# Merging a grouped attention's set-up blocks, loading by need, and moving the expert outputs' gathers and weight fetches

## The chip, the cores and the metric

The kernel runs on one core of one Trainium2 chip, as one launch. The metric is the device time of that launch in microseconds. Runs of the same kernel agree closely here: the three runs of the kernel before lie between 3903.95 and 3909.45 us.

A core has five engines with queues of their own: PE (TensorE, matmul), DVE (VectorE), ACT (ScalarE), POOL (GpSimd) and SP (SyncE, which here only issues transfers). They meet through semaphores. Each queue is worked in order, so an instruction that waits holds up everything behind it on its engine.

## The reference, cut to what matters

The input `x` is 4 batches of 256 tokens of 256 numbers; `ctx_2048` is 4 batches of 1601 rows of 256. Eight layers run one after the other, each as `x = x + layer(layernorm(x))`:

```python
x = x + _L0_xattn_ref(...)      # top-k memory attention
x = x + _L0_ffn_ref(...)        # 8 gelu experts, top 2 of them for each token
x = x + _L1_xattn_ref(...)      # grouped attention with rope
x = x + _L1_ffn_ref(...)        # linear
x = x + _L2_xattn_ref(...)      # image and text attention
x = x + _L2_ffn_ref(...)        # capacity experts
x = x + _L3_xattn_ref(...)      # grouped attention without rope
x = x + _L3_ffn_ref(...)        # silu experts
```

The gelu experts (`_L0_ffn_ref`): a softmax over 8 gates, and for each token the two largest, then

```python
h = gelu(x @ W1 + b1);  h = gelu(h @ W2 + b2);  eo = h @ W3 + b3
out = sum over the two chosen experts of  gate weight * eo
```

A grouped attention (`_L1_xattn_ref`, `_L3_xattn_ref`): 16 query heads of 128, 4 key and value heads. Queries come from `x`, keys and values from the context (in layer 1 from context and `x` together, 1857 rows). Queries and keys are RMS-normalised; layer 1 turns them by position (rope). Then softmax(q k / sqrt(128)) v, and the output projection.

## The kernel before

**Stages.** The layers are the stages a0, f0, a1, f1, a2, f2, a3, f3, and each consists of blocks. A block is a program for each engine; at its end all engines meet at a barrier, the semaphores are cleared, and they meet again. `x` stays in on-chip memory (`m.x`, in the profile `x_slots`) as 8 tiles of 128 tokens. The context lies in device memory as two halves, `ctx_hi` and `ctx_lo`, since each product is made of three products of high and low parts.

**f0, the gelu experts** (`gelu_experts`). The router gives each of the 2048 pairs (token, expert) a slot. POOL scatters the normalised rows to `z_slots` in device memory (L1665, 16 transfers), after which 15 blocks of 256 slots are worked (L1727, L1743, L1759 are the three layers' matmuls). For each block SP loads the rows (L1687, `f_zb`) and POOL fetches the expert's weights by index (L1641, 2.1 MB, three buffers). POOL fetches the weights of block 0 ahead of the scatters and those of blocks 1 and 2 directly behind them; then it rounds a third of block 0's weights (L1651), and DVE makes the low part of it (L1848) ahead of the low part of the first rows (L1853), which the first matmul needs. SP stores each block's results to `y_slots` (L1697). When all are stored, still in the same block, POOL gathers 16 tiles (expert choice `k`, token tile `t`) back (L1678, `got`, eight buffers), and DVE adds each to `x` times its gate weight (L1934).

**a1 and a3, the grouped attentions** (`grouped_attention`). Each has four blocks.

- `_once`: SP loads the norms' weights, the first weights and (in a1) the frequencies (L762) and waits for all; POOL sets constants (L768 to L774).
- `_first`: prepares batch 0's first key and value head. SP loads the whole context of batch 0 (L831, 1.6 MB for each half), then in a1 the positions (L822 to L826), then the tokens (L844, `a_x_n`). The order of work on the other engines is one list, `FIRST_TASKS`.
- `_groups`: 16 groups (4 batches of 4 heads) of 30 turns (a1) or 26 (a3). The list `GROUP_TURNS` says what is done beside the attention proper in each turn: the next head's keys and values, and so on.
- `_last`: the last output projection.

**Tasks** in the lists, a letter code with a number: `V` and `W` split weights into high and low; `PR`, `PX`, `RA` and `RS` make the table of sines and cosines from the positions (DVE L1353, L1357, L1370 to L1387, ACT L1136); `N`, `NZ`, `NX` normalise tokens; `KV t` is keys and values of context tile t (PE L929, ACT L1086 and L1088, DVE L1235); `KN` (POOL L1160 to L1165) and `KR` (DVE L1248 to L1256) normalise and turn four such tiles; `Q`, `QN`, `QR` the same for the queries; `KX` and `QX` transpose; `R` is a rough product of queries and keys and its maximum (PE L1002, DVE L1316, POOL L1188); `NB` spreads the maxima. Every engine does its own part of each task in the order of the list. Items that pass through PSUM (`PX NX KV Q KX QX OX Y NB`) share two banks in turn: item i waits until DVE has freed item i-2.

In `_first` R8 needs all keys (`KX3`), so the block is two parts: everything up to R8, and then R8 to R15 and NB0, which is a chain of PE and DVE alone. Groups begin after that.

## Time and profile before

| | us |
|---|---|
| median of three runs | 3904.76 |
| the runs | 3903.95, 3904.76, 3909.45 |
| the profiled execution | 3914.25 |
| its span, first to last instruction | 3912.1 |
| its mean granted TensorE clock, share of full | 0.936 |
| PE busy | 3534.0 (90%) |
| DVE busy | 2346.7 (60%) |
| ACT busy | 2243.7 (57%) |
| POOL busy | 853.5 (22%) |

The profile is one execution, so sums are made against its own 3914.25 us. Where PE is busy nearly without a break, only less work on PE would help; where PE stands idle, the engine or transfer that is waited for sets the time. On the page the span is cut into 40 slices, and a digit is the busy share of a slice in tenths:

```profile
PE   6756965999999999999599999886999999999989
DVE  8873756676676677664477777433555555555434
PEclk7866986999999999999799999887999999999989
```

### The profile page before, as it was taken

To read this page: it belongs to the slowest core of one execution; us is meant where nothing else is said; L and a number is where in the kernel's file an instruction comes from. 1 tells how busy PE (TensorE), PEld (TensorE's weight loads), DVE (VectorE), ACT (ScalarE), POOL (GpSimd) and SP (SyncE) were. 2 spreads that over 40 slices of the span, in tenths; PEclk is the share of its full clock that TensorE was granted. 3 is DMA by queue.
4 is the path that set the end of the run, shared out by engine and by line. 5 is a ranking of instruction groups with operands and counts; after the bars stand their busy time and mean duration, and the time that the engine had idled before them with its cause. 6 is when DMAs were issued, how large, how long until landed. Compare 5 with 4: busy or idle time off the path is not lost. (4 is left out here: it accounts for less than half of the span.)

```text
span 3912.1 us, 63758 instructions
## 1 busy us (share of the span) xinstructions
PE 3534.0 (90%) x23965; PEld 3018.9 (77%) x23965; DVE 2346.7 (60%) x4208; ACT 2243.7 (57%) x5207; POOL 853.5 (22%) x1073
## 2 busy tenths in 40 slices
PE   6756965999999999999599999886999999999989
PEld 5545964988988888888556666574898998989878
DVE  8873756676676677664477777433555555555434
ACT  3313743667666667666266666513666666666643
POOL 0002122222322222221111220102223232322214
PEclk7866986999999999999799999887999999999989
DMA  3213531010010001000200000101010010010001
GB/s 134 84 41 143 197 116 60 23 54 17 20 59 15 23 20 53 20 6 6 71 35 35 1 35 1 70 35 68 25 54 20 28 54 28 20 56 17 7 29 40
DMA packets 53360, 177.85 MB, mean 45 GB/s; under 512 B 5884, under 2 KB 27840, under 8 KB 46016
## 3 DMA queue, kind: packets, MB, share of 16 engines
q1 hardware_dynamic: 47200, 136.37, 9.9%
q0 software_dynamic: 3696, 35.72, 2.6%
q8 instruction: 192, 3.15, 0.3%
q10 hardware_dynamic: 2160, 1.71, 0.2%
q14 instruction: 112, 0.92, 0.1%
HBM read 145.44 MB, written 24.13 MB: 43 GB/s over the span
## 5 line engine op out<-in xcount | busy, mean ns | idle before, releaser
L1038 PE MATMUL ps<-a_v_rows,a_probs 128*128 128x129 f32 (+1 forms) x7168 | 943.8, 276 | 0.0
L1038 PEld LDWEIGHTS ps<-a_v_rows,a_probs 128*128 128x128 f32 (+1 forms) x7168 | 895.4, 191 | 39.9 <-issue 4.2
L1121 ACT ACTIVATE a_probs<-ps 128x512 f32<-128x512 f32 (+1 forms) x896 | 535.7, 598 | 605.4 <-PE ps L1027 604.4
L1316 DVE TENSOR_REDUCE a_neg<-ps 128x1 f32<-128x1024 f32 (+2 forms) x512 | 540.0, 1056 | 401.2 <-PE ps L1002 400.6
L1131 ACT ACTIVATE ps<-a_negb 128x512 f32<-128x512 f32 (+1 forms) x892 | 536.7, 602 | 58.2 <-DVE a_negb L1331 30.2
L1188 POOL TENSOR_SCALAR a_diag<-ident,a_negmax 128x128 fp32r<-128x128 f32 x256 | 157.9, 617 | 1482.2 <-DVE a_negmax L1324 1480.6
L1023 PE MATMUL ps<-a_qt,a_kt 128*128 128x512 f32 (+1 forms) x896 | 428.4, 478 | 1.4 <-PEq L72 1.4
L929 PE MATMUL ps<-a_wr,a_ct 128*128 128x256 f32 (+1 forms) x2496 | 363.1, 287 | 10.1 <-DVE a_k_rows L1235 7.8
L929 PEld LDWEIGHTS ps<-a_wr,a_ct 128*128 128x128 f32 (+1 forms) x2496 | 335.6, 187 | 37.9 <-DVE a_k_rows L1235 10.2
L1027 PE MATMUL ps<-a_qt,a_kt 128*128 128x512 f32 (+1 forms) x896 | 355.5, 397 | 0.0
L1025 PE MATMUL ps<-a_qt,a_kt 128*128 128x512 f32 (+1 forms) x896 | 354.1, 395 | 0.0
L3238 ACT ACTIVATE a_probs<-ps 128x1024 f32<-128x1024 f32 x224 | 229.6, 1025 | 151.2 <-PE ps L3117 150.8
L1002 PE MATMUL ps<-a_kt,a_qt 128*128 128x512 f32 (+2 forms) x1024 | 292.8, 369 | 13.8 <-DVE a_negmax L1324 6.8
L1235 DVE TENSOR_TENSOR a_k_rows<-ps,a_kw 128x128 f32<-128x128 f32 (+1 forms) x448 | 129.6, 290 | 213.5 <-ACT a_v_rows L1088 201.0
L3416 DVE TENSOR_REDUCE a_parts<-ps 128x1 f32<-128x448 f32 x384 | 222.9, 618 | 46.9 <-PE ps L3079 44.9
L1002 PEld LDWEIGHTS ps<-a_kt,a_qt 128*128 128x128 f32 x1024 | 178.5, 193 | 70.6 <-DVE a_neg L1316 26.7
L1027 PEld LDWEIGHTS ps<-a_qt,a_kt 128*128 128x128 f32 (+1 forms) x896 | 165.7, 185 | 42.9
L1023 PEld LDWEIGHTS ps<-a_qt,a_kt 128*128 128x128 f32 (+1 forms) x896 | 170.0, 190 | 4.8 <-issue 2.8
L1025 PEld LDWEIGHTS ps<-a_qt,a_kt 128*128 128x128 f32 (+1 forms) x896 | 169.2, 189 | 0.8
L3117 PE MATMUL ps<-a_qt,a_kt 128*128 128x512 f32 x448 | 165.0, 450 | 2.2 <-DVE a_qt L3408 1.2
L3079 PE MATMUL ps<-a_kt,a_qt 128*128 128x448 f32 (+1 forms) x512 | 154.6, 371 | 7.5 <-ACT a_kt L3206 1.6
L1161 POOL TENSOR_TENSOR a_k_sq<-a_k_sq,nhalf 128x4 f32<-128x4 f32 (+2 forms) x128 | 151.2, 1181 | 10.7
(461 smaller groups left out, 6048.9 us busy)
## 6 DMA issues: line engine op xcount, KB each, us to landing
a_ct<-ctx_hi SPq DMA_DIRECT2D x12, 1602.0 KB, 6.9
a_ct<-ctx_lo SPq DMA_DIRECT2D x12, 1602.0 KB, 10.6
a_wf<-in_a_wq SPq DMA_DIRECT2D x32, 512.0 KB, 3.5
a_wf<-in_a_wo SPq DMA_DIRECT2D x32, 512.0 KB, 3.5
f_we<-in_f_experts SPq DMA_DIRECT2D x8, 1088.0 KB, 8.7
a_wf<-in_a_wkv SPq DMA_DIRECT2D x32, 256.0 KB, 2.7
ctx_hi<-a_ct SPq DMA_DIRECT2D x4, 1602.0 KB, 5.3
ctx_lo<-a_ct SPq DMA_DIRECT2D x4, 1602.0 KB, 8.8
```

What stands on the lines that cost most here:

```text
L929: ins = pe.matmul(out[0:r, 0:2 * HD], src, wr[0][v][:, c * 2 * HD:(c + 1) * 2 * HD], start=(n == 0), stop=(n == 3 * DC - 1))
L1002: ins = pe.matmul(m.ps[:, rough_at(task) + k, 0:c1 - c0], queries[0][:, j * P:(j + 1) * P], keys[0][:, c0:c1], start=True, stop=True)
L1023: pe.matmul(out, kt[0][:, at:at + r], qt[0][:, cols], start=False, stop=False, skip_group_check=True)
L1025: pe.matmul(out, kt[0][:, at:at + r], qt[1][:, cols], start=False, stop=False, skip_group_check=True)
L1027: pe.matmul(out, kt[1][:, at:at + r], qt[0][:, cols], start=False, stop=True, skip_group_check=True).then_inc(st_ready, 1)
L1038: ins = pe.matmul(m.ps[:, 6 + i // 2, (i % 2) * 256:(i % 2) * 256 + VW], probs[0:r, n % 3, i * P:(i + 1) * P], v_rows[g % 2][0:r, t, :], s ...
L1121: act.activation(probs[0:r, n % 3, :], m.ps[0:r, 4 + n % 2, :], ACT.Exp)\
L1131: act.activation(m.ps[0:r, 4 + n % 2, :], negb[0:r, G, :], ACT.Copy).then_inc(seeded, 1)
L1316: ins = dve.tensor_reduce(neg2[:, j, r % 2:r % 2 + 1], flat2(m.ps[:, rough_at(task):rough_at(task) + 2, :])[:, 0:e - a0], AX.X, ALU.max, n ...
L3117: ins = pe.matmul(m.ps[:, 4 + 2 * (n % 2) + half, :], kt[g % 2][:, half, t * P:(t + 1) * P], qt[g % 2][:, half, :], start=True, stop=True)
L3238: act.activation(flat2(probs[n % 3][:, :, :]), flat2(m.ps[:, first:first + 2, :]), ACT.Exp)\
L3416: dve.tensor_reduce(to, slot(("R", h, j))[:, 0:n], AX.X, ALU.max, negate=True).then_inc(neg_done, 1)
```

## The change

**In f0.** POOL's fetch of block 1's weights waits until the rows of block 0 have landed, and the fetch of block 2's until those of block 1 have. The gathers and additions at the end of f0 are taken out; the slots and the gate weights (one copy on DVE, `share`) are kept for the next stage.

**In a1.** The gathers and additions are done by two new tasks, `GP j` on POOL and `GA j` on DVE, j from 0 to 15, with four buffers (halves of `z` and `x_b`) in place of eight. The first four pairs, which make batch 0's tokens, are in `FIRST_TASKS`; the other twelve are in group 0's turns 8 to 21 of `GROUP_TURNS`.

**In a1 and a3.** The block `_once` is gone; its loads and constants are the head of `_first`. POOL sets only the last context tile of `k_rows`, not all. SP's loads come in a new order, the context in two column parts (512 columns and the rest) with a semaphore each; `KV4` waits for the second. In `_first` the items use four PSUM banks, not two (`_groups` keeps two). `FIRST_TASKS` is another order.

The lists, of which the tables' rows themselves tell little:

```diff
 GROUP_TURNS = {
     True: (
-        "KV4 RA1 R4", "KV5 KV6 KN0 QR3", "R5 KV7 KR0 KN1", "Y0 KR1 KV8 W1 R6", "KV9 KX0", "R7 KV10 KV11 KR2",
...
+        "KV4 RA1 R4", "KV5 KV6 KN0 QR3", "GP4 R5 KV7 KR0 KN1", "GP5 Y0 KR1 KV8 W1 R6", "GP6 KV9 KX0 GA4",
...
 FIRST_TASKS = {
     True: (
-        "V1 V0 PR0 N0 PX0 RA0 RA1 RA2 RA3 NZ0 RA4 NX0 RA5 RA6 RA7 RA8 RA9 Q0 Q1 RS0 KV0 QN0 KV1 KV2 KV3 KV4 QR0 "
...
+        "GP0 V0 GP1 PR0 GP2 PX0 RA0 RA1 RA2 RA3 GA0 RA4 GA1 RA5 RA6 GA2 RA7 GP3 KV0 GA3 RA8 RA9 KV1 KV2 N0 KV3 "
...
     False: (
-        "V1 N0 V0 NZ0 NX0 Q0 Q1 KV0 KV1 KV2 KV3 KV4 KV5 KV6 QN0 KV7 KV8 KN0 QN1 KN1 KV9 KV10 KV11 KV12 QX0 KN2 KX0 "
...
+        "N0 V0 KN0 NZ0 QN0 QN1 KV0 NX0 KV1 V1 KV2 KV3 Q0 Q1 KN1 KX0 KV4 KV5 KV6 KV7 KV8 KV9 KV10 KV11 W1 KN2 QX0 "
```

The code:

```diff
-        with nc.Block(name=f"{name}_once") as block:
-            @block.sync
-            def _(sp):
-                loads = [(qw[:, :], w["qw"].partition_broadcast(P)), (kw[:, :], w["kw"].partition_broadcast(P)),
-                         (wf[0][:, :], w["wkv"][0]), (wf[1][:, :], w["wq"][0])]
...
-                sp.wait_ge(once, 16 * len(loads))
...
+            ITEM_BANKS = (2, 3) if attend else (2, 3, 6, 7)
...
                     if not attend:
-                        load_context(0)
+                        load_weights(KVH - 2, 0)
+                        sp.dma_start(qw[:, :], w["qw"].partition_broadcast(P)).then_inc(norm_in, 16)
+                        sp.dma_start(kw[:, :], w["kw"].partition_broadcast(P)).then_inc(norm_in, 16)
                         if rope:
+                            sp.dma_start(invf[:, :], w["inv_freq"].partition_broadcast(P)).then_inc(norm_in, 16)
+                            sp.wait_ge(zeroed, 1)
                             load_positions(0)
-                        sp.dma_start(x_n[:, :, :], m.x[:, 0:QT, :]).then_inc(x_in, 16)
+                        else:
+                            sp.dma_start(x_n[:, :, :], m.x[:, 0:QT, :]).then_inc(x_in, 16)
+                        load_context(0, 0)
+                        load_weights(KVH - 2, 1)
+                        load_context(0, 1)
+                        if rope:
+                            sp.wait_ge(m.added, 2 * QT)
+                            sp.dma_start(x_n[:, :, :], m.x[:, 0:QT, :]).then_inc(x_in, 16)
...
+                    def GP(g, j):
+
+                        k, t = PAIRS[j]
+                        if j >= 4:
+                            pool.wait_ge(m.added, j - 3)
+                        pool.indirect_dma_start(out=got(j), out_offset=None, in_=m.y_slots,
+                                                in_offset=bass.IndirectOffsetOnAxis(ap=m.slot[:, k, t:t + 1], axis=0))\
+                            .then_inc(m.fetched[j % 4], 16)
...
+                    def GA(g, j):
+
+                        k, t = PAIRS[j]
+                        dve.wait_ge(m.fetched[j % 4], 16 * (j // 4 + 1))
+                        if k:
+                            dve.wait_ge(m.added, j)
+                        dve.scalar_tensor_tensor(out=m.x[:, t, :], in0=got(j), scalar=m.share[:, t, k:k + 1],
+                                                 in1=m.x[:, t, :], op0=ALU.mult, op1=ALU.add).then_inc(m.added, 1)
...
+                    if not attend:
+                        dve.wait_ge(zeroed, ZEROED)
+                        dve.wait_ge(norm_in, 16 * NORMS)
...
+                pool.wait_ge(z_in[0], 16)
                 fetch_weights(1)
+                pool.wait_ge(z_in[1], 16)
                 fetch_weights(2)
...
-                for i in range(2):
-                    pool.wait_ge(y_out[i], 16 * len(range(i, NB, 2)))
-                for j, (k, t) in enumerate(fetches):
-                    if j >= 8:
-                        pool.wait_ge(added, j - 7)
-                    pool.indirect_dma_start(out=got[:, j % 8, :], out_offset=None, in_=m.y_slots,
-                                            in_offset=bass.IndirectOffsetOnAxis(ap=slot[:, k, t:t + 1], axis=0))\
-                        .then_inc(fetched[j % 8], 16)
```

**Where instructions stand on the queues.** First SP, from the end of f0 into a1's first block; in brackets is what an instruction waits for. The kernel before:

```order
L1633 UNCONDITIONAL_BRANCH [waits f0_y_out1,f0_y_out0]
L71 ISA [waits barrier_Pool_Activation_PE_DVE_SP_release] x2
L755 UNCONDITIONAL_BRANCH [waits barrier_Pool_Activation_PE_DVE_SP_release]
L762 DMA a1_qw<-in_a1_qw 128x128
L762 DMA a1_kw<-in_a1_kw 128x128
L762 DMA a1_wf0<-in_a1_wkv 128x512
L762 DMA a1_wf1<-in_a1_wq 128x1024
L762 DMA a1_invf<-in_inv_freq 128x64
L754 UNCONDITIONAL_BRANCH [waits a1_once]
L71 ISA [waits barrier_Pool_Activation_PE_DVE_SP_release]
L818 UNCONDITIONAL_BRANCH [waits barrier_Pool_Activation_PE_DVE_SP_release]
L831 DMA a1_ct0<-ctx_hi 128x3204
```

The changed kernel, SP at the same place:

```order
L805 UNCONDITIONAL_BRANCH [waits barrier_Pool_Activation_PE_DVE_SP_release]
L826 DMA a1_wf0<-in_a1_wkv 128x512
L831 DMA a1_qw<-in_a1_qw 128x128
L832 DMA a1_kw<-in_a1_kw 128x128
L834 DMA a1_invf<-in_inv_freq 128x64
L809 DMA a1_pos_i<-in_pos 12x128 [waits a1_zeroed]
L811 DMA a1_pos_i<-in_pos 1x65
L813 DMA a1_pos_i<-in_tok 2x128
L820 DMA a1_ct0<-ctx_hi 128x2x512
L820 DMA a1_ct1<-ctx_lo 128x2x512
L826 DMA a1_wf1<-in_a1_wq 128x1024
L820 DMA a1_ct0<-ctx_hi 128x2x1090
```

The barrier between the two lists of loads is gone, and the positions stand ahead of the context; before, they stood behind both of its loads.

Next POOL in f0, from the scatters on (`expert_in0` is the arrival of block 0's weights). Before:

```order
L1665 DMA z_slots<-f_z,f_slot 3840x256 x15
L1641 DMA f_wf<-in_f_experts,f_of 128x4104 x2
L1651 CAST f_wr<-f_wf 128x1024 [waits expert_in0]
L1651 CAST f_wr<-f_wf 128x1024 [waits f0_h_ready,expert_in1]
L1641 DMA f_wf<-in_f_experts,f_of 128x4104 [waits f0_hi_done,f0_w_lo]
```

And in the changed kernel:

```order
L1701 DMA z_slots<-f_z,slot 3840x256 x15
L1677 DMA f_wf<-in_f_experts,f_of 128x4104 [waits f0_z_in0]
L1677 DMA f_wf<-in_f_experts,f_of 128x4104 [waits f0_z_in1]
L1687 CAST f_wr<-f_wf 128x1024 [waits expert_in0]
L1687 CAST f_wr<-f_wf 128x1024 [waits f0_h_ready,expert_in1]
```

The two fetches now wait for rows (`z_in`), and the rounding of block 0's weights, which waits for neither, stands behind them.

Last POOL in group 0 of a1, turns 7 to 13 (the three lines on `a_k_sq` and `a_k_rows` are one `KN`, the line on `a_diag` is an `R`). Before:

```order
L1165 TENSOR_TENSOR a_k_rows<-a_k_rows,a_k_sq 128x512
L1188 TENSOR_SCALAR a_diag<-ident,a_negmax 128x128
L1160 TENSOR_SCALAR a_k_sq<-a_k_sq 128x4
L1161 TENSOR_TENSOR a_k_sq<-a_k_sq,nhalf 128x4
L1165 TENSOR_TENSOR a_k_rows<-a_k_rows,a_k_sq 128x512
L1188 TENSOR_SCALAR a_diag<-ident,a_negmax 128x128
L1160 TENSOR_SCALAR a_k_sq<-a_k_sq 128x4
L1161 TENSOR_TENSOR a_k_sq<-a_k_sq,nhalf 128x4
```

And changed:

```order
L1170 TENSOR_TENSOR a_k_rows<-a_k_rows,a_k_sq 128x512
L1201 DMA a_z<-y_slots,slot 128x256
L1193 TENSOR_SCALAR a_diag<-ident,a_negmax 128x128
L1165 TENSOR_SCALAR a_k_sq<-a_k_sq 128x4
L1166 TENSOR_TENSOR a_k_sq<-a_k_sq,nhalf 128x4
L1170 TENSOR_TENSOR a_k_rows<-a_k_rows,a_k_sq 128x512
L1201 DMA a_z<-y_slots,slot 128x256
L1201 DMA a_x_b<-y_slots,slot 128x256 x2
L1193 TENSOR_SCALAR a_diag<-ident,a_negmax 128x128
L1201 DMA a_z<-y_slots,slot 128x256 x2
L1165 TENSOR_SCALAR a_k_sq<-a_k_sq 128x4
```

Six gathers now stand among two `KN` and two `R` steps; the two directly ahead of the last `KN` shown are GP8 and GP9, and GP9 waits for the addition GA5 on DVE.

## Rows read from the trace of the kernel before

**Rows 1.** Busy time by stretch: from:to, length, engines' busy, clock, DMA share, GB/s

```profile
core 0: us, PE busy (x) PEld busy (x) DVE busy (x) ACT busy (x) POOL busy (x), PEclk, DMA share, GB/s
340.00:355.00 15.00, 0.64 (x3) 0.67 (x4) 1.22 (x1) 0.00 (x0) 2.81 (x3) 0.50 0.84 324
556.00:581.00 25.00, 0.00 (x0) 0.00 (x0) 7.75 (x16) 0.00 (x0) 15.16 (x16) 0.52 0.29 84
589.30:665.80 76.50, 38.59 (x149) 28.08 (x149) 49.26 (x85) 20.26 (x75) 17.99 (x22) 0.63 0.15 57
```

**Rows 2.** Timeline, f0's first rows: start, length, engine, line, [idle before, releaser]

```profile
339.82 0.98 POOL L1641 DMA_INDIRECT f_wf<-in_f_experts,f_of  x1 [0.30 <-issue]
340.96 14.87 SPq L1687 DMA_DIRECT2D f_zb<-z_slots  x3
342.07 1.05 POOL L1651 CAST f_wr<-f_wf 128x1024 fp32r<-128x1024 f32 x1
343.16 1.22 DVE L1848 TENSOR_TENSOR f_wr<-f_wf,f_wr 128x1024 fp32r<-128x1024 f32 x1 [13.55 <-POOL f_wr L1651]
354.36 1.09 PE L1712 MATMUL ps<-ident,f_zb 128*128 128x128 f32 x4 [27.48 <-DMA f_zb<-z_slots]
356.95 5.46 PE L1727 MATMUL ps<-f_zt_b,f_wr 128*128 128x256 f32 x24 [1.50 <-DVE f_zt_b L1853]
...
365.32 1.07 ACT L1803 ACTIVATE f_wr<-f_wf 128x1024 fp32r<-128x1024 f32 x1
```

**Rows 3.** Line L1687, the 15 loads of rows: time to landing

```profile
DMA to landing us min/median/max: 2.6/6.6/13.4
```

**Rows 4.** Timeline, the end of f0 and the start of a1

```profile
556.41 0.97 POOL L1678 DMA_INDIRECT f_got<-y_slots,f_slot  x1 [18.16 <-DMA y_slots<-f_yb]
...
559.22 0.48 DVE L1934 SCALAR_TENSOR_TENSOR x_slots<-f_got,f_top,x_slots 128x256 f32<-128x256 f32 x1 [5.23 <-DMA f_got<-y_slots,f_slot]
...
577.96 0.48 DVE L1934 SCALAR_TENSOR_TENSOR x_slots<-f_got,f_top,x_slots 128x256 f32<-128x256 f32 x1 [0.82 <-DMA f_got<-y_slots,f_slot]
581.02 0.35 SPq L762 DMA_DIRECT2D a_qw<-in_a_qw  x1
...
582.84 0.43 SPq L762 DMA_DIRECT2D a_invf<-in_inv_freq  x1
```

**Rows 5.** Line L762, the nine loads of both once blocks: time to landing

```profile
DMA to landing us min/median/max: 2.9/4.5/5.8
```

**Rows 6.** Timeline, a1's first block

```profile
601.00 0.21 DVE L1353 CAST a_pos_rows<-a_pos_i 15x128 f32<-15x128 int32 x1 [8.68 <-DMA a_pos_i<-in_tok]
...
602.86 1.17 DVE L1370 TENSOR_TENSOR a_ang_tmp<-a_pos_f,a_invf 128x960 f32<-128x960 f32 x1
```

**Rows 7.** Busy time from first angle (a1) or token statistics (a3) to R8

```profile
602.86:650.72 47.86, 28.21 (x130) 22.91 (x130) 34.31 (x62) 17.81 (x73) 14.64 (x18) 0.71 0.00 1
2669.86:2700.66 30.80, 20.63 (x116) 16.25 (x116) 12.45 (x31) 14.17 (x64) 13.19 (x18) 0.83 0.08 26
```

**Rows 8.** Transfers by line, whole span: issues, KB each, median us to landing

```profile
a_x_n<-x_slots SPq DMA_DIRECT2D x8, 256.0 KB, 2.3
```

**Rows 9.** Timeline, a3's once and first blocks

```profile
2650.54 0.33 SPq L762 DMA_DIRECT2D a_qw<-in_a_qw  x1
...
2669.86 0.75 DVE L1222 BATCH_NORM_STATS2 a_stats<-a_x_n 128x6 f32<-128x256 f32 x2 [9.75 <-DMA a_x_n<-x_slots]
```

**Rows 10.** Busy time in group 0 of a1

```profile
665.90:734.00 68.10, 67.99 (x454) 61.13 (x455) 43.58 (x76) 47.90 (x125) 19.36 (x24) 0.97 0.12 40
```

**Rows 11.** Timeline, one KN on POOL in group 0 of a1

```profile
700.93 0.19 POOL L1160 TENSOR_SCALAR a_k_sq<-a_k_sq 128x4 f32<-128x4 f32 x1
...
702.75 1.04 POOL L1165 TENSOR_TENSOR a_k_rows<-a_k_rows,a_k_sq 128x512 f32<-128x512 f32 x1
```

**Rows 12.** Timeline in f0, a weight fetch beside DVE's splits

```profile
422.27 0.95 POOL L1641 DMA_INDIRECT f_wf<-in_f_experts,f_of  x1 [0.48 <-issue]
422.48 2.36 DVE L1848 TENSOR_TENSOR f_wr<-f_wf,f_wr 128x1024 fp32r<-128x1024 f32 x2 [0.40 <-ACT f_wr L1803]
```

109 lines of the change are left out of this document (58 added, 51 removed), and 9 rows, old and new, of tables (FIRST_TASKS, GROUP_TURNS).

## The prediction

> **What bounds the kernel now.** I read the busy shares by slice first: PE is at nine tenths in most slices, and the dips lie between stages. So the time is PE's work plus the stretches in which PE stands still, and the change touches three of these. The table of busy time by stretch [rows 1] shows them: 15 us at the start of the experts in which PE does 0.64 us of work; 25 us at their end with none; and a1's first block, 76.5 us with PE at 38.6 and DVE at 49.3. The timelines then say what each waits for.
>
> In the first [rows 2], SP issues block 0's rows at 340.96, and PE starts on them at 354.36: a wait of 13.4 us, in which the DMA engines move 324 GB/s on average [rows 1], nearly all of it the two weight fetches issued from 339.82. The same load takes 2.6 us at best and 6.6 in the middle of the 15 [rows 3].
>
> In the second [rows 4], POOL has waited for the last store until 556.41, gathers 16 tiles one after the other, and DVE adds the last at 577.96. Next comes the once block from 581.02, whose loads must all land before the first block begins. There the angles begin only at 602.86, because the positions, queued behind 3.2 MB of context, are used first at 601.00 [rows 6]. The a3 stage shows the same: from 2650.54 to the first use of the tokens at 2669.86 nothing but loads is on the path [rows 9].
>
> **Part 1, the weight fetches.** With the rows alone in flight they land 2.6 us after 340.96, at 343.6. This releases POOL, which issues both fetches (0.97 each and 0.3 between: to 345.9) and only then rounds block 0's third part (1.05, to 347.0); DVE's low part follows (1.22, to 348.3), and only behind it the low part of the rows. From the rows' arrival PE needed 356.95 - 354.36 = 2.59 us to its first expert matmul [rows 2], so the rows' own chain would be done at 346.2; the rounding is the later one. With an estimated 0.7 for the rows' low part, a transfer-free piece of that 2.59, the first matmul starts at 349.0, against 356.95: **-7.9**. The new wait holds back, on POOL, both fetches and the rounding, and PE waits for all three in the end. Block 1's weights now start 3.8 us later and land, if both share the engines as they did, some 13 us after 343.6, at 357. ACT splits them first at 365.32 [rows 2], 357.4 when 7.9 is taken off, so there is no margin: up to 3 us can be lost here. One copy on DVE (`share`) adds about 0.2. Part 1: **-7.7**, between -9 and -4.
>
> **Part 2, the end of f0 and the start of a1.** From the last addition's end, 577.96 + 0.48 = 578.44, to the next block's first instruction took 2.6 us [rows 4]. Without the tail the same barriers start when the last store has landed, at 556.4 (the cause of POOL's release), so a1 begins at 559.0 in place of 581.02: **-22.0**. This holds within 0.5 us, since it is an interval of the trace with its content taken out.
>
> From a1's first load to the first angle it was 602.86 - 581.02 = 21.8 us. Now frequencies are the fourth load, 1.4 us after the start at the measured spacing of 0.45, and the norms' loads took 2.9 to 5.8 us to land, 4.5 in the middle [rows 5]. DVE waits for all of them before anything else: 5.9. Then a split half as wide as the 1.22 one of [rows 2], some 0.7, and the cast, transposition and copy of the positions, at most the 602.86 - 601.00 = 1.9 us that they took with the tokens' statistics between [rows 6], say 1.2: the angles begin 7.8 us in. **-14.0**, between -12.5 and -16. The positions are issued by about 3 us, and are tiny, so they aren't last; the context is behind them now, and KV0 needs only its first 512 columns. The four gathers issue on POOL while it has nothing else to do, 1.25 us each, and land before DVE, busy with angles, asks for them: no cost but their additions.
>
> From the first angle to R8 it was 47.86 us, with DVE busy 34.31 and PE 28.21 [rows 7]: neither is full, it is a chain that passes between them. DVE gets four additions (4 x 0.48), two splits of 1.2 that stood outside this stretch and the tokens' statistics (0.75 [rows 9] and small steps, some 1.2): 5.5 more, 39.8. If DVE were never idle, the stretch would be 39.8 (-8.0); if its idle 13.55 us stayed as they are, 53.4 (+5.5). The new order fills some of that idle time: KV0 to KV3 run on PE under the angles, where PE was waiting, and four banks let PE run ahead of DVE. Against it: tokens now wait for the fourth addition and a 2.3 us copy [rows 8], and Q comes late, so that POOL's QN and KN1 follow one another. I followed DVE's list by hand with the durations of this trace and came to 46; it is near the middle, and I take **-2.0**. R8 to the groups' start keeps its work.
>
> **Part 3, a3.** From the once block's first load to the tokens' use it was 19.3 us [rows 9]. Now the tokens are the fourth load (1.4 us in) ahead of the context; the copy takes 2.3 us alone [rows 8] and up to the 5.8 of such loads behind 384 KB. I take 5.5 in all: **-13.8**, between -12 and -15. From there to R8 it was 30.8 us with PE at 20.63 and DVE at 12.45 [rows 7]. Two banks made PE wait for DVE; four don't. One split (1.2) comes in. From PE's floor (-10) to the same idle time (+1.2); I take **-2.0**, nearer to the upper end, because Q, its norm on POOL and the keys' norms behind it on POOL are still one chain.
>
> **Part 4, group 0 of a1.** PE is busy 67.99 of 68.10 us there, DVE 43.58, POOL 19.36 [rows 10]. Twelve gathers take POOL 12 x 0.95 and twelve additions DVE 12 x 0.48 = 5.8 us. Both have room, but the queues are in order. Most exposed is KN2, which ran from 700.93 to 703.79 [rows 11]: POOL must now first issue GP8 and GP9, and GP9 waits for GA5 on DVE, which stands behind KR2. That puts KN2 about 3 us later, DVE's KR4 behind it 1 to 2 us, and PE's next item behind DVE about 1. With a similar smaller slip elsewhere: **+2**, between 0 and +9 (every addition on the path, and KN2's 3 us).
>
> **A rule against part 4.** The fetch at 422.27 kept its 0.95 us on POOL although DVE worked on a split, two operands from SBUF, from 422.48 for 2.36 us [rows 12]. The Trainium skill ("SBUF — State Buffer", section "SBUF: two separate sides") says that a transfer issued from GpSimd needs descriptors written by GpSimd, and that DVE, while it holds the shared port pair in a two-port mode, keeps GpSimd from writing them; so the transfer waits for the end of DVE's instruction. By it, gathers issued among DVE's rope products would each come up to a DVE instruction late, which is the second rival's direction; in the row the issue itself isn't longer. The sum stays with the row.
>
> **Sum:** -7.7 - 22.0 - 14.0 - 2.0 - 13.8 - 2.0 + 2 = **-59.5 us**. On the profiled 3914.25 that is 3854.8. The median of the runs is 9.5 us lower than the profiled execution, and no row ties this difference to the changed places, so I take the same sum off the median: 3904.76 - 59.5 = **3845.3**.
>
> **Rivals.**
> 1. *The rows are late for another reason than the weights* (the scatters just before them write the same memory). Then the fetches, which now wait for the rows, start at 354.4, the rounding ends 3.4 us later, and the first matmul comes at 359.8: +2.9 in place of -7.7. Time 3855.9. Against it: the 324 GB/s, and the 2.6 us of an undisturbed load. 5%.
> 2. *Group 0 pays for each gather.* POOL is in order, and PE follows DVE closely: if each of twelve gathers costs PE its issue and gap, 1.25 us, part 4 is +15. Time 3858.3. For it: PE has no slack at all [rows 10]. Against it: POOL and DVE have. 8%.
> 3. *Slower: the ring of four runs empty.* If DVE reaches each GA before its gather has landed, it waits for a whole round: from POOL's issue to DVE's start 2.8 us, the addition 0.48, 0.3 of issue [rows 4], and where a KN or R stands between on POOL its 2.9 as well [rows 11]. This is 6.5 us for each of twelve, 78 in all, PE behind it: 3904.76 - 61.5 + 78 = 3921. It decides from 61.5 / 12 = 5.1 us for each. Against it: the turns are 2.3 us long (68.1 / 30) and GA stands two turns behind its GP, with three more gathers in flight. 2%.
> 4. *The first blocks gain nothing in their order*: the idle time stays (+5.5 and +1.2 in place of -2.0 twice), 3856. Within my range, part of the forecast.
>
> **How the numbers follow.** The forecast with its unknown terms has 83%, the rivals 5, 8 and 2, and 2 for what I don't see. The terms' ends add up to gains between 40 and 75 us if not all fall to one side: 3830 to 3865, which holds rivals 1 and 2; I give 3832 to 3864. A change of 0.2% (7.8 us) is about what a measurement of this kernel can tell from none. Faster by more: 0.97; within: 0.01; slower: 0.02.
>
> **What would show it.** In the profile after: block 0's rows landing 2.6 to 4 us after their issue, and PE's first expert matmul about 8 us after that issue (16 before); POOL's rounding behind both fetches; no gathers ahead of the barrier, and a1's first load 2.6 us behind the last store's landing; the first angle 8 us later; R8 about 54 us after a1's first load (69.7 before) and, in a3, about 34 (50.1 before); KN2 in group 0 ending some 3 us later in its group, and the group 2 us longer than 68. Wrong would be: a stall of ACT on block 1's weights, DVE waiting at the start of the first block for norms' loads over 7 us, a longer stretch from angles to R8, or DVE waiting on gathers in group 0.

## The result and the profile after

The changed kernel takes 3838.14 us (median of 4 runs, 3836.81 to 3841.64), the kernel before 3904.36 beside it (3903.17 to 3909.45). The ratio is 0.9829, 95% interval 0.9812 to 0.9846: 66.2 us, or 1.7%, less. Forecast were 59.5 less (3845.3). The profiled execution took 3837.82, with a span of 3836.1.

Its timeline where f0's experts start answers to [rows 2]. Columns are start, length, engine, line, operation, and in brackets the idle time before and its releaser:

```profile
336.13 4.17 SPq L1717 DMA_DIRECT2D f_zb<-z_slots  x3
338.82 1.09 PE L1742 MATMUL ps<-ident,f_zb 128*128 128x128 f32 x4 [16.78 <-DMA f_zb<-z_slots]
338.95 0.98 POOL L1677 DMA_INDIRECT f_wf<-in_f_experts,f_of  x1 [4.26 <-DMA f_zb<-z_slots]
340.23 0.96 POOL L1677 DMA_INDIRECT f_wf<-in_f_experts,f_of  x1 [0.30 <-issue]
341.20 1.04 POOL L1687 CAST f_wr<-f_wf 128x1024 fp32r<-128x1024 f32 x1
342.28 1.23 DVE L1878 TENSOR_TENSOR f_wr<-f_wf,f_wr 128x1024 fp32r<-128x1024 f32 x1 [17.51 <-POOL f_wr L1687]
343.42 0.68 DVE L1883 TENSOR_TENSOR f_zt_b<-ps,f_zt_b 128x512 fp32r<-128x512 f32 x1
344.25 4.74 PE L1757 MATMUL ps<-f_zt_b,f_wr 128*128 128x256 f32 x24 [4.34 <-DVE f_zt_b L1883]
...
351.92 1.07 ACT L1833 ACTIVATE f_wr<-f_wf 128x1024 fp32r<-128x1024 f32 x1
```

The rows are in PE's hands 2.7 us behind their issue, where they took 13.4. What remains until the first expert matmul is POOL's list: two fetches, one rounding, then DVE's two low parts. Block 1's weights land 8.6 us behind their fetch's issue, at 347.6, and ACT splits them from 351.92, without a wait.

The end of f0 and the start of a1 answer to [rows 4] and [rows 6]:

```profile
540.55 0.36 SPq L1727 DMA_DIRECT2D y_slots<-f_yb  x1
543.82 0.35 SPq L826 DMA_DIRECT2D a_wf<-in_a_wkv  x1
...
549.28 0.69 DVE L1226 TENSOR_TENSOR a_wr<-a_wf,a_wr 128x512 fp32r<-128x512 f32 x1 [8.76 <-DMA a_invf<-in_inv_freq]
550.58 0.21 DVE L1387 CAST a_pos_rows<-a_pos_i 15x128 f32<-15x128 int32 x1 [0.60 <-DMA a_pos_i<-in_tok]
551.38 1.15 DVE L1404 TENSOR_TENSOR a_ang_tmp<-a_pos_f,a_invf 128x960 f32<-128x960 f32 x1
```

No gather stands ahead of the barrier, and the angles begin 7.56 us behind a1's first load. Busy time by stretch: the first two rows answer to [rows 7] (first angle to R8 in a1, token statistics to R8 in a3), the third to [rows 10] (the first 68.1 us of group 0). Columns as in [rows 1]:

```profile
551.38:593.86 42.48, 25.24 (x130) 21.84 (x130) 37.81 (x71) 18.32 (x73) 16.65 (x18) 0.70 0.29 106
2596.34:2624.89 28.55, 17.53 (x112) 15.57 (x112) 13.01 (x32) 14.07 (x64) 14.17 (x18) 0.80 0.43 155
608.57:676.67 68.10, 66.06 (x434) 58.88 (x435) 47.31 (x85) 46.14 (x122) 32.90 (x35) 0.96 0.19 63
```

DVE is now busy 37.81 of 42.48 us in a1's first stretch, where it stood idle for 13.55 us before. In group 0, PE has lost 1.9 us.

I cut both traces, and later those of the experiments, at the same events. All values are lengths in us, the difference of two starts read in the timeline (B and C meet at the end of the last copy of outputs):

| stretch | before | changed | difference | forecast |
|---|---|---|---|---|
| A rows' issue to first expert matmul | 15.99 | 8.12 | -7.9 | |
| B to the last output copy's end | 197.03 | 196.27 | -0.8 | A and B: -7.7 |
| C to a1's first load | 27.04 | 3.30 | -23.7 | -22.0 |
| D to the first angle | 21.84 | 7.56 | -14.3 | -14.0 |
| E to R8 | 47.86 | 42.48 | -5.4 | -2.0 |
| F to the groups' first score | 15.19 | 14.71 | -0.5 | 0 |
| G to a1's last score | 1200.89 | 1202.47 | +1.6 | +2 |
| H a3's first load to token statistics | 19.32 | 4.64 | -14.7 | -13.8 |
| I to R8 | 30.80 | 28.55 | -2.3 | -2.0 |
| J to the groups' first score | 15.08 | 14.18 | -0.9 | 0 |

These add up to -68.8. The spans differ by 76.0; the other 7.2 lie where nothing was changed: everything ahead of the rows' issue took 4.8 us less, a1's last score to a3's first load 3.1 less, and what follows a3's first score 0.7 more. Over the 14 traces of this study these two stretches vary from 336.1 to 341.4 and from 776.8 to 785.0 us, so they say nothing about a change. The profiled execution of before (3914.25) lay 9.9 us above its median, that of the changed kernel 0.3 below; the medians, 66.2 apart, are the measure.

### The profile page after: what moved, and what is told of

It is laid out like the page before. It is cut to its first block and busy times, and to the rows that moved or that the text cites. A ratio compares the mean times of both kernels' runs of the same rounds, so it can differ in the third digit from the quotient of the medians.

```text
span 3836.1 us, 63738 instructions
## 1 busy us (share of the span) xinstructions
PE 3525.6 (92%) x23965; PEld 3014.9 (79%) x23965; DVE 2343.7 (61%) x4209; ACT 2240.2 (58%) x5207; POOL 855.4 (22%) x1073
## 3 DMA queue, kind: packets, MB, share of 16 engines
q1 hardware_dynamic: 53600, 136.37, 10.1%
```

## The experiments

All were run beside the kernel before, which took 3909.7 to 3911.4 us there; so ratios are compared, and stretches by the letters above. A second profile of the changed kernel says how exact a stretch is.

**The changed kernel again.** 

> The changed kernel once more, beside the combined version on the same chip. Its ratio to the kernel before should fall in 0.981 to 0.985, and the stretches of its trace should agree with the first profile's within 1 us: 8.1 us from the rows' issue to the first expert matmul, 64 to 66 from a1's first load to its groups, 1202.5 for them, 47.4 from a3's first load to its groups. If a stretch differs by more, differences of that size in the other experiments mean nothing.

Median 3842.70, ratio 0.9823 (0.9809 to 0.9836). A 8.20, B 196.03, C 3.30, D 7.73, E 42.29, F 14.72, G 1202.68, and a3's H to J together 47.23 where the first profile had 47.37. These stretches repeat within 0.4 us (H and I each for itself shift by 0.4 and 0.5, their sum by 0.1). In the experiments below D varies between 7.3 and 8.5 without an edit to it, so D is good to about 1 us. Where the interval of a ratio overlaps the repeat's, as in all experiments but 3, 4 and 5, it is the stretches that tell, not the time.

**1. The weights in front of the rows.** 

> The changed kernel without POOL's two waits for the first rows: weight fetches 1 and 2 are issued right behind the scatters, as before the change. Theory (the small load of rows is served in turns with 4 MB of weights): rows land 12 to 14 us after their issue instead of 2.7, the first expert matmul comes 16 us behind the issue instead of 8.1, the time is 7 to 9 us above the changed kernel's, about 3846. Rival (the rows were late because of the scatters just ahead of them, and come early in the changed kernel for another reason): they land in about 3 us here too, and the time stays at 3838.

```diff
-                pool.wait_ge(z_in[0], 16)
                 fetch_weights(1)
-                pool.wait_ge(z_in[1], 16)
                 fetch_weights(2)
```

Ratio 0.9837 (0.9818 to 0.9857). The timeline of its start:

```profile
338.73 15.38 SPq L1715 DMA_DIRECT2D f_zb<-z_slots  x3
...
352.63 1.08 PE L1740 MATMUL ps<-ident,f_zb 128*128 128x128 f32 x4 [28.00 <-DMA f_zb<-z_slots]
...
355.22 5.03 PE L1755 MATMUL ps<-f_zt_b,f_wr 128*128 128x256 f32 x22 [1.50 <-DVE f_zt_b L1881]
```

The rows take 13.9 us again, and A is 16.49, 8.3 more than in the repeat. Everything else is as in the changed kernel. The rival (the scatters make the rows late) falls: the scatters stand ahead of them in both kernels, and only the two waits differ. The ratios alone, 5 us apart, with intervals that overlap, couldn't have told it.

**2. The once block put back.** 

> The changed kernel with a once block put back ahead of the heads' first block in all grouped attentions (norms' weights, first key and query weights, frequencies, memsets, all waited for, then a barrier); the order of the other loads and of the tasks stays. Theory (the order of the loads did most of the work in a1, the second wait and barrier the rest): in a1 the first angle comes 11 to 12 us behind the first load (7.6 in the changed kernel, 21.8 before), in a3 the tokens' statistics 10 to 11 us behind it (4.6; 19.3 before), in all +9 us, about 3847. Rival (the once block itself was the cost): a1 back at over 18 us and a3 at over 16, in all +22 or more.

```diff
+        with nc.Block(name=f"{name}_once") as block:
+            @block.sync
+            def _(sp):
+                loads = [(qw[:, :], w["qw"].partition_broadcast(P)), (kw[:, :], w["kw"].partition_broadcast(P)),
+                         (wf[0][:, :], w["wkv"][0]), (wf[1][:, :], w["wq"][0])]
...
+                sp.wait_ge(norm_in, 16 * len(loads))
...
+        st.clear()
```

The block also sets all of `k_rows` again, as before the change. D is 11.22 (+3.5 on the repeat), H 10.29 (+5.3); the ratio is 0.9839 (0.9823 to 0.9856), median 3847.45. So the wait for all loads and the barrier are worth 9 us in the two stages together. The remaining 20 of D and H are taken to come from what stands ahead of what; this is a remainder, not a run of its own.

**3. The gathers back in f0.** 

> The changed kernel with all 16 gathers and additions put back at the end of the experts' block, as before; everything else stays. Theory (the tail was a serial stretch of its own and its work costs little inside a1): from the last store's issue to a1's first load 26 to 27 us instead of 3.3, the first block of a1 1 to 2 us shorter, group 0 of a1 1.5 us shorter, in all +20 to +22, about 3859. Rival (the gathers cost a1 several us, which other gains hide): a1's first block and group 0 become over 5 us shorter and the whole is under +17.

The edit puts POOL's wait for `y_out`, its 16 gathers and DVE's 16 additions back behind the loop over blocks, and takes all GP and GA out of a1's lists.

Ratio 0.9877 (0.9861 to 0.9894), 0.0054 or 21 us above the repeat. C is 27.04, exactly that of before. D is 7.26, E 39.72 (2.6 less than the repeat), F 15.07, G 1201.65 (1.0 less). The tail was worth 23.7 us, and its work costs a1 2.7 us in the first block (D to F), more than the 1 to 2 expected and than the additions alone, which were all I had counted, and 1.0 us in G; group 0 by itself lost more than that, as part 4 below shows.

**4. The first tasks in nearly the old order.** 

> The changed kernel with the heads' first tasks in nearly the order they had before the change (both splits first, queries ahead of the keys), the four first gathers and additions ahead of the tokens; loads, banks and all else stay. Theory A (the new order fills DVE's and PE's idle time): the stretch from the first angle to R8 in a1, 42.5 us in the changed kernel, goes to 48 to 52, and in a3 the stretch from the tokens' statistics to R8, 28.6 us, grows by 2 to 4: in all +8 to +12. Theory B (the shorter stretch comes from the four banks, the new order does nothing of its own): both stay within 1.5 us.

```diff
-        "GP0 V0 GP1 PR0 GP2 PX0 RA0 RA1 RA2 RA3 GA0 RA4 GA1 RA5 RA6 GA2 RA7 GP3 KV0 GA3 RA8 RA9 KV1 KV2 N0 KV3 "
...
+        "GP0 V1 GP1 V0 PR0 GP2 PX0 RA0 RA1 RA2 RA3 GA0 RA4 GA1 RA5 RA6 GA2 RA7 GP3 GA3 N0 RA8 RA9 NZ0 NX0 "
+        "Q0 Q1 RS0 KV0 QN0 KV1 KV2 KV3 KV4 QR0 "
...
```

In a1 this is not the old list exactly: the tokens' tasks N0, NZ0 and NX0 stand behind RA7, since the tokens are now loaded last.

Ratio 0.9880 (0.9863 to 0.9896): 22 us above the repeat, twice what theory A expected; theory B falls. D is 15.70, E 54.17, F 15.21: from a1's first load to its groups 85.1 us, against 84.9 in the kernel before. With nearly the old order, all that the loads, the banks and the single block gain in a1 is lost to the four gathers and to waits. In a3 H is 13.20 and H to J 55.69 (+8.5); the stretch in which theory A looked for a3's loss, I, did not grow (27.40). Two rows of its timeline show how:

```profile
559.61 1.83 DVE L1227 TENSOR_TENSOR a_wr<-a_wf,a_wr 128x1024 fp32r<-128x1024 f32 x2 [16.45 <-ACT a_wr L1074]
...
580.69 5.25 PE L948 MATMUL ps<-a_wr,a_zt 128*128 128x512 f32 x12 [1.50 <-DVE a_zt L1240]
```

V1, the split of the query weights, is DVE's first task. Its weights are loaded behind 1 MB of context (two parts of 512 KB), so DVE stands until 559.61, 13.2 us behind the first load; in the changed kernel the positions are in use 6.8 us behind it. Then PE's first large work is Q, at 580.69, at the lower clock. In the changed kernel Q comes behind keys:

```profile
569.78 2.99 PE L947 MATMUL ps<-a_wr,a_zt 128*128 128x512 f32 x12
```

The busy time of these two intervals, the changed kernel's first, then this one's; the third number from the end is the granted clock:

```profile
569.78:572.77 2.99, 2.99 (x15) 2.40 (x15) 1.76 (x6) 1.68 (x11) 0.00 (x0) 0.99 0.27 101
```

```profile
580.69:585.94 5.25, 5.25 (x14) 4.14 (x15) 0.69 (x1) 1.15 (x8) 0.00 (x0) 0.53 0.00 0
```

0.99 is the level of 2.4 GHz; 0.53 is for the most part that of 1.2. Ahead of 580.69 PE had been busy for 1.4 of the 19.7 us since 561.00; ahead of 569.78 it had been busy for 11.5 of the 15.5 us since 554.26. The same twelve matmuls take 2.3 us more at the lower clock. In the kernel before they took as long as in this one:

```profile
610.14 5.29 PE L944 MATMUL ps<-a_wr,a_zt 128*128 128x512 f32 x12 [1.58 <-DVE a_zt L1216]
```

**5. Old order and gathers in f0.** 

> Both undone at once: the heads' first tasks in nearly the old order, and all gathers back at the end of the experts' block; the single block, the loads by need and the four banks stay. Theory (the old order is bad only because the tokens now come late, behind four additions, and Q stands ahead of the keys): from a1's first load to its groups 73 to 78 us, against 84.9 before, 85.1 with the old order and gathers in a1, and 62.1 with the new order and no gathers. Rival (the old order costs as much without gathers): 82 to 85.

The edits are those of 3 and 4 together. Ratio 0.9930 (0.9915 to 0.9945). D 14.47, E 49.77, F 15.54: 79.8 us, between theory and rival. DVE stands for V1 here as well. The four corners for a1's first load to its groups are then:

| | gathers in f0 | gathers in a1 |
|---|---|---|
| nearly the old order | 79.8 | 85.1 |
| new order | 62.1 | 64.8 |

With the new loads, the order is worth 17.7 us without gathers and 20.3 with them. Loads by need, the single block and four banks together, with nearly the old order, are worth 84.9 - 79.8 = 5.1. The new order with the old loads was not run.

**6. Two banks.** 

> The changed kernel with two banks of PSUM for the items of the heads' first block instead of four. Theory A (four banks let PE run ahead of DVE and are part of the gain): from the first angle to R8 in a1 3 to 6 us longer than 42.5, from the tokens' statistics to R8 in a3 2 to 3 us longer than 28.6, in all +5 to +9. Theory B (the order alone does it, the chain passes through POOL and DVE): both within 1 us of the changed kernel.

```diff
-            ITEM_BANKS = (2, 3) if attend else (2, 3, 6, 7)
+            ITEM_BANKS = (2, 3)
```

Ratio 0.9844 (0.9828 to 0.9861). E 48.92 (+6.6), a3's H to J 49.22 (+2.0). Theory A holds, with 0.6 more in a1 than expected and less in a3's I (+1.5 for 2 to 3). The table of PE's waits shows the mechanism; in this kernel, from 556 to 605 us (line waited for: us in total, times, longest):

```profile
PE ps L932 <- DVE a_k_rows L1267: 8.9, 6, 3.9
```

and in the changed kernel, from 551 to 594:

```profile
PE ps L932 <- DVE a_k_rows L1267: 1.6, 2, 1.1
```

PE's keys wait until DVE has emptied a bank: DVE is busy with the angles, and with four banks the program lets PE work up to four tiles ahead of it.

**7. POOL's rounding ahead of the waits.** 

> The changed kernel with POOL's rounding of block 0's third part ahead of both waits for rows, where in the changed kernel it stands behind both fetches. Theory (POOL's fetch, fetch, rounding and then DVE's two low parts are the chain to the first expert matmul): that matmul comes 5.3 to 5.7 us behind the rows' issue instead of 8.1, the time falls by 2.5 to 3, about 3835.5. Rival (PE then waits for block 1's weights or for the clock, so the start is given back): the first matmul is earlier, but from the rows' issue to f0's last copy of outputs stays 204.4 us.

```diff
+                split_third(0)
                 pool.wait_ge(z_in[0], 16)
                 fetch_weights(1)
...
-                    split_third(b)
+                    if b:
+                        split_third(b)
```

Ratio 0.9815 (0.9799 to 0.9832). A is 5.42, B 197.16; together 202.6 against 204.2 in the repeat. The matmul comes 2.8 us earlier as expected, and in this trace 1.1 us of that are lost again in B; in two later versions with the same edit A and B are 201.3 and 201.8, a gain of 2.4 to 2.9. What took them here stays open.

**8. A smaller first load of the context.** 

> The changed kernel with the first load of the context cut from 512 columns to 256 and 256, each with its own semaphore. Theory (PE stands still for the context's low part first: 3.1 and 1.6 us in a1, to 9.5 us behind the first load in a3): KV0 starts about 3 us earlier in a1 and 4 us earlier in a3, and R8 comes 1 to 3 us earlier in a3, up to 1 us in a1, where DVE's list is full: -2 to -4 in all. Rival (the chain through the tokens, Q and POOL's norm sets R8): KV0 is earlier and R8 is not, within 0.5 us.

```diff
-                        cols = slice(0, 512) if part == 0 else slice(512, CTXP)
+                        cols = (slice(0, 256), slice(256, 512), slice(512, CTXP))[part]
...
```

Ratio 0.9818 (0.9800 to 0.9837). In a3 PE starts its keys 6.96 us behind the first load, not 9.2 to 9.5, and H to J is 44.82 (-2.4). In a1 they start at 9.14 (9.6 and 10.4 in the two profiles of the changed kernel), and E stays at 42.26: there DVE is the one that is full. This is what a load by need left over. In the changed kernel's a3 the wait moved from the tokens to the context:

```profile
2596.34 0.75 DVE L1254 BATCH_NORM_STATS2 a_stats<-a_x_n 128x6 f32<-128x256 f32 x2 [5.36 <-DMA a_x_n<-x_slots]
...
2601.19 1.62 PE L932 MATMUL ps<-a_wr,a_ct 128*128 128x256 f32 x6 [12.05 <-DMA a_ct<-ctx_lo]
```

**9. Group 0's gathers later, two per turn.** 

> The changed kernel with the twelve gathers and additions of group 0 moved from turns 8 to 21 to turns 15 to 22, behind KN2 and KN3, and the copy of x behind them. Theory (KN2 behind the gathers on POOL costs group 0 its 1.6 us): KN2 ends 38 us behind the groups' start (42 in the changed kernel), and from the groups' start in a1 to its last score it takes 1200.9 as before instead of 1202.5: -1 to -2 us. Rival (each gather and addition costs PE wherever it stands): the stretch stays at 1202.5 or grows, since two gathers stand in each turn.

```diff
-        "GP11 KN3 QX1 GA9", "GP12 KR6 KX1 KR7 KX2 GA10", "GP13 RA3 RA4 GA11", "GP14 KX3 GA12", "GP15 RA5 GA13",
...
+        "KN3 QX1 GP4 GP5", "GP6 KR6 KX1 KR7 KX2 GP7", "GP8 RA3 RA4 GA4 GA5 GP9", "GP10 KX3 GA6 GA7 GP11",
+        "GP12 RA5 GA8 GA9 GP13", "GP14 R8 GA10 GA11 GP15", "R9 RA6 GA12 GA13", "R10 RA7 RA8 GA14 GA15",
```

Ratio 0.9826 (0.9810 to 0.9842): no gain and no loss. Its profile shows G at 1208.02, 5.3 more than the repeat, with one hole: ACT stands until 672.16, DVE until 673.57, PE until 674.84, and what released them is not in the trace:

```profile
672.16 0.60 ACT L1125 ACTIVATE a_probs<-ps 128x512 f32<-128x512 f32 x1 [3.06 <-remote]
...
673.57 1.22 DVE L1351 TENSOR_REDUCE a_neg<-ps 128x1 f32<-128x1024 f32 x1 [4.36 <-remote]
```

No other profile here has such a hole. PE stands 4.5 us in it, and from 672 to 680 us the granted clock is 0.60. The profiled execution was also the longest of the four (3852.31 against a median of 3843.75), so G tells nothing. Up to the hole the theory holds: KN2 ends 38.5 us behind the groups' start, as expected, and POOL's product of KN3 starts at 44.4, where it starts at 44.5 without gathers (experiment 3) and at 48.3 in the changed kernel. Whether the gathers then cost PE something in their new turns this run can't say; the next two can.

**10. A combined version.** 

> Four things on top of the changed kernel: POOL's rounding of block 0's third part ahead of the waits for rows; the context's first 512 columns in two loads; in a1 the frequencies and positions are the first loads, the positions' cast and angles stand ahead of the first split, which alone waits for the norms; group 0's gathers one per turn in turns 14 to 25 with their additions two to three turns behind, the copy of x last. Expected: first expert matmul 5.4 us behind the rows' issue (8.1), in a1 the first angle 5 to 6 us behind the first load (7.6 to 8.4) with R8 following by 2, group 0 to the last score 1201 (1202.5), a3's first load to its groups 44.8 (47.4); in all 7 to 8 us below the changed kernel. Rival: DVE, full in a1's first block, gives back what the angles gain, and one gather per turn still stalls the ring in group 0 as two did; then only 4 us, or less, remain.

```diff
-        "GP0 V0 GP1 PR0 GP2 PX0 RA0 RA1 RA2 RA3 GA0 RA4 GA1 RA5 RA6 GA2 RA7 GP3 KV0 GA3 RA8 RA9 KV1 KV2 N0 KV3 "
+        "GP0 PR0 GP1 PX0 GP2 V0 RA0 RA1 RA2 RA3 GA0 RA4 GA1 RA5 RA6 GA2 RA7 GP3 KV0 GA3 RA8 RA9 KV1 KV2 N0 KV3 "
...
-        "GP11 KN3 QX1 GA9", "GP12 KR6 KX1 KR7 KX2 GA10", "GP13 RA3 RA4 GA11", "GP14 KX3 GA12", "GP15 RA5 GA13",
...
+        "KN3 QX1 GP5", "KR6 KX1 KR7 KX2 GP6", "RA3 RA4 GP7 GA4", "KX3 GP8 GA5", "RA5 GP9 GA6",
+        "R8 GP10 GA7", "GP11 R9 RA6 GA8", "R10 RA7 RA8 GP12 GA9", "GP13 RA9 R11 GA10",
+        "RS0 R12 GP14 GA11", "GP15 R13 GA12", "R14 GA13", "R15 W0 NX0 GA14", "NB0 GA15", "XC0",
```

Median 3837.65, ratio 0.9814 (0.9801 to 0.9828). Against the repeat A and B are 2.9 shorter, a3's H to J 1.7, and G is 1199.42, 3.3 shorter, nearly all of it in group 0 (part 4 below). With one gather per turn behind KN2, PE is full again in the first 68 us of group 0:

```profile
608.49:676.59 68.10, 68.00 (x455) 61.13 (x456) 47.33 (x85) 47.95 (x126) 32.29 (x36) 0.98 0.19 59
```

But a1's first block takes 66.6 us, 1.9 more. Its timeline:

```profile
544.87 0.22 DVE L1393 CAST a_pos_rows<-a_pos_i 15x128 f32<-15x128 int32 x1 [6.34 <-DMA a_pos_i<-in_tok]
545.46 0.17 DVE L1397 COPY a_pos_f<-ps 128x15 f32<-128x15 f32 x1 [0.38 <-PE ps L911]
549.66 0.69 DVE L1232 TENSOR_TENSOR a_wr<-a_wf,a_wr 128x512 fp32r<-128x512 f32 x1 [4.02 <-DMA a_kw<-in_a_kw]
550.26 1.15 DVE L1410 TENSOR_TENSOR a_ang_tmp<-a_pos_f,a_invf 128x960 f32<-128x960 f32 x1
```

The positions are there 3.0 us behind the first load (541.84), and DVE then waits 4.0 us for the norms' weights, the wait for which I had put in front of the split. The first to need them is the keys' tile, at 559.00; a wait placed there wasn't tried.

**11. Angles first.** 

> The combined version of e9 with two repairs in a1's first block: the split of the first key weights, which waits for the norms' loads, stands behind the first two angle tasks instead of ahead of them, and the context's last part is loaded ahead of the first query weights. Theory (in e9 the wait for the norms only took the place of the wait for the positions, and the context's last part was late behind the weights): the first angle comes 3.8 to 4.3 us behind the first load (8.4 in e9, 7.6 to 8.4 in the changed kernel), PE's second wait for the context (3.4 us) is gone, and a1's first load to its groups takes 62 to 63.5 us against 66.6 in e9 and 64.8 in the changed kernel; the ratio to the kernel before is 0.9805. Rival (Q's chain through POOL sets R8, and the query weights are late now): 65 us or more, ratio 0.9815 as e9.

The e9 of this text is the combined version of experiment 10, and the lists are shown against it:

```diff
-        "GP0 PR0 GP1 PX0 GP2 V0 RA0 RA1 RA2 RA3 ...
+        "GP0 PR0 GP1 PX0 GP2 RA0 RA1 V0 RA2 RA3 ...
...
```

D is 4.34, at the end of what was expected, but E is 45.71, so that D to F are 64.8, equal to the changed kernel: 1.9 better than the version before, 1.3 above the theory's upper end. After two angle tasks DVE waits again for the norms (2.06 us), and PE's wait for the context's last part is down from 3.4 to 2.2 us. Median 3833.28, ratio 0.9799 (0.9786 to 0.9813), the lowest of all. Its interval still touches the repeat's (0.9809 to 0.9836), and the stretches give 5.0 us of gain (A and B 2.4, G 1.0, a3 1.6), so it is probably faster than the changed kernel, by some 5 to 9 us. The list of group 0 is that of experiment 10, whose G was 2.3 lower.

## Why the prediction was right, and where it was off

**Part 1 (-7.7) was right, and its mechanism is shown.** The chain came as worked out: 8.12 us from the issue, where 349.0 - 340.96 = 8.04 was forecast. Experiment 1 turns it back. The loss feared for block 1's weights didn't come, because the sum had a wrong time for them: they land 8.6 us behind the issue, not some 13, which leaves 4.4 us until ACT takes them. In the kernel before it was the second fetch, block 2's, that took 12.9 us; the first took 8.5.

**Part 2, the tail (-22.0), was 1.7 us too small.** I took the 2.6 us between the last addition and the next block for the price of the barrier. In the kernel before the last store is issued at

```profile
554.01 0.36 SPq L1697 DMA_DIRECT2D y_slots<-f_yb  x1
```

and lands 2.1 us later, 0.3 ahead of POOL's next step at 556.41 [rows 4]. In the changed kernel it lands in 2.1 us as well, and a1's first load stands 3.27 us behind its issue: 1.1 us for barrier and clearing, not 2.6. The trace's records of the barrier say where the rest was. From POOL's first step in it to the next block's first load it is 0.93 us in both kernels. But in the kernel before DVE is done at 578.49 and POOL takes that first step at 580.09. These 1.6 us stand in both traces that have the gathers at the block's end (before, and experiment 3) and not in the changed kernel's; what POOL does in them isn't in the trace, so their cause stays open. "Within 0.5 us" was too sure: the interval held something that went with the gathers.

**Part 2, to the first angle (-14.0), was right, and came by the path worked out:** DVE stands 5.5 us for the norms' loads (5.9 forecast), its split takes 0.7, and 1.4 us behind the split the angles begin (1.2 forecast). What the sum didn't show is how much of it hangs on the list. By experiment 5, with those loads and nearly the old order, D is 14.5: half of the gain (21.8 to 14.5) comes with the loads and the single block alone, the other half (14.5 to 7.3, without gathers) needs a list that V1 no longer heads. I had seen that only one split stands ahead of the positions, and priced it by its duration, 0.7 us, not by the load that the other split would have waited for.

**Part 2, angle to R8 (-2.0), is the term of the sum that was mis-sized:** -5.4, and -0.5 behind R8. The forecast of 46 us left DVE 6.2 us idle beside 39.8 of work; it had 37.8 of work and 4.7 idle. The text gave the banks and the order together -2. The runs give the banks 6.6 alone; the order 10.1 (49.77 to 39.72, without gathers); and the four gathers and additions 2.6 against it. These don't add up to -5.4, since each is taken back from the changed kernel, and nearly the old order with the new loads (49.77) is slower than the kernel before (47.86). Part of the order's gain is the clock: Q runs at 0.99 and takes 2.99 us, where it took 5.29 in the kernel before. No row of the kernel before was used for that, though the granted clock of the stretch, 0.71 [rows 7], was there to be read.

**Part 3 (-13.8 and -2.0) came at -14.7 and -2.3,** with 0.9 more behind R8. The tokens took 4.64 us for 5.5. Here too the new loads need the new list: with nearly the old one H is 13.2, not 4.6. The new wait that the sum didn't name is the one for the context's first part, 9.5 us behind the first load; experiment 8 shows that it cost 2.4 us.

**Part 4 (+2) came at +1.6 in G, by the mechanism named, but group 0 itself lost 3.2.** KN2 ends 42.0 us behind the groups' start, not 37.9: 4.1 later, for about 3 forecast. POOL's list there, then DVE's wait:

```profile
646.65 0.95 POOL L1201 DMA_INDIRECT a_z<-y_slots,slot  x1 [0.51 <-DVE x_slots L1248]
...
649.56 1.04 POOL L1170 TENSOR_TENSOR a_k_rows<-a_k_rows,a_k_sq 128x512 f32<-128x512 f32 x1
```

```profile
650.63 0.69 DVE L1280 TENSOR_TENSOR a_by_sin<-a_k_rows,a_cs 128x512 f32<-128x512 f32 x1 [2.07 <-POOL a_k_rows L1170]
```

And PE behind it:

```profile
652.31 0.66 PE L968 MATMUL ps<-ident,a_q_rows 128*128 128x128 f32 x4 [1.46 <-DVE a_k_rows L1267]
```

G holds 16 groups, and only group 0 was edited. Cut at the start of POOL's first `a_k_rows` product of the next group, the traces show (us):

| | groups' start to there | from there to a1's last score |
|---|---|---|
| before | 92.5 | 1108.4 |
| changed, and the repeat | 95.7, 95.6 | 1106.7, 1107.1 |
| no gathers in a1 (experiments 3 and 5) | 93.2, 92.8 | 1108.5, 1108.5 |
| gathers behind KN2, one per turn (10 and 11) | 92.4, 93.3 | 1107.1, 1108.5 |

So the twelve gathers where the change put them cost 2.3 to 3.1 us (92.8 and 93.2 against 95.5 to 95.9 in the changed kernel and all experiments that keep this list), and moved behind KN2 they cost nothing that shows. In the unedited rest the traces differ by about 1.6 us, for a reason that the runs don't show. That this went against the loss in group 0 made +1.6 out of +3.2: in part the nearness to +2 is luck.

**The rivals.** The first (rows late for another reason) is refuted by experiment 1. The second (1.25 us of PE for each gather) would be 15 us; it was 2.3 to 3.1. The third (the ring runs empty) didn't happen: in group 0 of the changed kernel DVE waits for no gather. The fourth (the first blocks gain nothing in their order) is refuted: E and I became shorter, and with the new loads the order is worth 17.7 us or more in a1's first block.

So the total came within 7.2 us (3838.1 for 3845.3) because each gap closed about as far as its length in the trace allowed. Every term missed to the same side, so no error of one hid that of another; only inside G did that happen. What the sum had wrong is the worth of the list: whoever had taken over the loads and the banks and left nearly the old lists would have got 5.1 us in a1's first block without gathers, of the 22.8 that the whole gave there (84.9 to 62.1).

## What to carry to other kernels

When loads are put in the order of need, look first at what heads each engine's list: an engine that executes in order waits for the load of its first task, so a new load order with the old list can be worth little (5.1 of 22.8 us here). A small load in flight beside megabytes can pay for them (2.7 us alone, 13.4 and 13.9 beside two weight fetches); the wait that holds the large ones back cost nothing here, where the first of them still landed 4.4 us ahead of its use. After such a repair ask for the next load that PE waits for: in a3 it was the context's first part, and halving that load gave another 2.4 us; in a1, where DVE was full, it gave nothing. And cut a long stretch where the edit ends: G as a whole hid half of what group 0 lost.
